# A gated cross-attention and mixture-of-experts block on one core: expert rows added to the rows of x in DRAM by indirect transfers, in place of a store and a gather

## The reference

```python
x = x + tanh(g_xattn) * xattn(layernorm(x), ctx, masks)      # 16 heads, 128 context rows
n = layernorm(x)
probs, idx = top_k(softmax(n @ router), 2)                   # 8 experts, each token takes 2
routed = sum_k probs[k] * (silu(n @ gate[idx[k]]) * (n @ up[idx[k]])) @ down[idx[k]]
shared = (silu(n @ shared_gate) * (n @ shared_up)) @ shared_down
x = x + tanh(g_ffn) * (routed + shared)
```

## The kernel before, in words

| engine | in this order in iteration k |
|---|---|
| SP | load the 128 token numbers of slot k (L405), after the gather of slot k-4 |
| POOL | gather the normed rows of slot k (L514), after PE has transposed slot k-4 |
| PE | transposes of g_h, slot k-3; transposes of the gathered rows, slot k (both L1038); gate and up products, slot k-1; down product, slot k-3 (L1046 to L1048) |
| DVE | g_h_lo, slot k-2; g_lo, slot k (L964); g_y of slot k-3 (L970), the down product times its scale; g_h, its peak and scales, slot k-1 |
| ACT | g_ht, slot k-3; store of g_y of slot k-4 to `y_dram` (expert_rows), L651; g_h_hi, slot k-2; g_hi, slot k; silu, slot k-1 |

## Time and profile before

### The profile page before, as it was taken

One profiled execution on the slowest core, in us unless ns is written; L12 is line 12 of the kernel. 1 busy time (PEld: TensorE's weight loads), 2 busy tenths in 40 slices (PEclk: granted clock), 3 DMA queues, 4 the chain that ended last, 5 costly groups with the idle time before them and its releaser, 6 DMA issues.

```text
span 1155.8 us, 26617 instructions
## 1 busy us (share of the span) xinstructions
PE 1050.2 (91%) x7344; PEld 677.3 (59%) x7345; DVE 822.7 (71%) x2938; ACT 531.4 (46%) x1041; POOL 441.8 (38%) x654
## 2 busy tenths in 40 slices
PE   4699979999999999860899999999999999999997
PEld 3488767777777777660455555555554444444443
DVE  5899868788888888763576666666665666666666
ACT  1366546666666666640444444444443232232322
POOL 3254647676667667442112112112110423232322
PEclk9999889999999999855899999999999999999999
DMA  7555573223323223432233333333332544444543
GB/s 290 197 177 179 131 173 95 93 93 93 93 93 94 94 93 110 101 102 72 74 110 118 115 113 118 118 109 118 118 109 67 185 158 161 157 168 149 169 149 128
DMA packets 76731, 146.96 MB, mean 127 GB/s; under 512 B 20912, under 2 KB 23088, under 8 KB 73872
## 3 DMA queue, kind: packets, MB, share of 16 engines
q1 hardware_dynamic: 46512, 66.01, 20.0%
q10 hardware_dynamic: 17280, 44.83, 10.5%
q0 software_dynamic: 12896, 35.58, 9.9%
HBM read 94.04 MB, written 52.35 MB: 127 GB/s over the span
## 4 chain that ended last, share of the span: by engine, by line
PE 64%; issue 11%; DVE 9%; POOL 8%; ACT 4%; DMA 2%; POOLq 1%; another core or an unknown queue 1%; SPq 0%; DVEq 0%; ACTq 0%
PE bank L1046 15%; PE bank L1047 15%; PE bank L1048 15%; PE bank L1038 8%; PE bank L1090 3%; PE bank L1108 3%; DVE arena L776 3%; POOL arena L467 3%; POOL token_of_row L503 2%; ACT arena L605 1%; DVE arena L865 1%; POOL arena L474 1%; DMA token_of_row<-arena 1%; DVE peak L879 1%; PE bank L1064 1%
## 5 line engine op out<-in xcount | busy, mean ns | idle before, releaser
L1046 PE MATMUL bank<-weights,arena 128*128 (+1 forms) x682 | 259.9, 381 | 2.1 <-ACT arena L647 1.9
L1047 PE MATMUL bank<-weights,arena 128*128 (+1 forms) x682 | 259.8, 381 | 0.0
L1048 PE MATMUL bank<-weights,arena 128*128 (+1 forms) x682 | 259.6, 381 | 0.0
L1038 PE MATMUL bank<-ident,arena 128*128 128x128 f32 (+1 forms) x1592 | 189.4, 267 | 56.1 <-DMA arena<-normed_rows,arena 25.7
L1038 PEld LDWEIGHTS bank<-ident,arena 128*128 128x128 f32 (+1 forms) x1592 | 161.4, 132 | 103.0 <-issue 71.9
L514 POOL DMA_INDIRECT arena<-normed_rows,arena x71 | 67.1, 946 | 254.9 <-PE bank L1038 238.7
L1108 PEld LDWEIGHTS bank<-arena 128*128 128x128 f32 x1024 | 131.7, 198 | 34.3 <-issue 29.5
L1090 PE MATMUL bank<-arena 128*128 128x512 f32 x256 | 138.8, 647 | 5.4 <-DVE arena L776 5.1
L1108 PE MATMUL bank<-arena 128*128 128x33 f32 x1024 | 128.8, 276 | 2.9 <-issue 1.8
L467 POOL TENSOR_TENSOR arena<-arena 128x512 f32<-128x512 f32 x96 | 101.3, 1056 | 76.8 <-DVE arena L776 75.7
L524 POOL DMA_INDIRECT arena<-expert_rows,arena x64 | 62.8, 981 | 173.9 <-DVE arena L998 156.1
(11 more groups left out here) (175 smaller groups left out, 1895.7 us busy)
## 6 DMA issues: line engine op xcount, KB each, us to landing
expert_rows<-arena ACTq DMA_DIRECT2D x71, 256.0 KB, 2.1
arena<-in_x SPq DMA_DIRECT2D x64, 256.0 KB, 3.2
weights<-in_w_gu ACTq DMA_DIRECT2D x8, 1024.0 KB, 4.7
x_rows<-arena SPq DMA_DIRECT2D x32, 256.0 KB
normed_rows<-arena SPq DMA_DIRECT2D x32, 256.0 KB, 4.9
normed_transposed<-arena SPq DMA_DIRECT2D x32, 256.0 KB, 2.3
arena<-normed_transposed SPq DMA_DIRECT2D x32, 256.0 KB, 3.3
arena<-x_rows SPq DMA_DIRECT2D x32, 256.0 KB, 3.4
```

The lines of the kernel that those rows point to most:

```text
L1038: last = t.transpose(dst[:, c * P:(c + 1) * P], src[:, c * P:(c + 1) * P], (ident16 if src.dtype == F16 else ident)[:, :])
L1046: t.matmul(dst, hi[:, rows], w_hi(c), start=(c == 0), stop=False)
L1047: t.matmul(dst, hi[:, rows], w_lo(c), start=False, stop=False)
L1048: last = t.matmul(dst, lo[:, rows], w_hi(c), start=False, stop=(c == chunks - 1))
```

## The change

Three things change together. (1) The list in DRAM has two words a row: token number and weight. Rows that nobody writes hold, in place of zero, one of 288 (SPARE) token numbers beyond the last token, with weight 0; `x1_dram` and `xn_dram` get 288 rows more, which POOL fills with zeros at the start. POOL therefore makes seven stores at the start instead of one. In the attention pass POOL copies the token number into both entries, DVE writes prob * gate beside them at L856 (where it now waits for the scatters of the tile two earlier), and the scatters carry 8 bytes a row. (2) In the expert pass DVE multiplies each row of the down product by its own weight (g_weight: the row's scale times the list's weight), and POOL, in place of ACT's store, adds the 128 rows to the rows of `x1_dram` by an indirect transfer with compute_op add. Each add is issued only once the one before it has landed, since two slots may hold the same token. (3) The last pass gathers nothing: x1 as loaded already holds the expert rows, and one DVE operation makes the result. SP waits for all adds before it loads x1; the five plan operations for row_all go.

```diff
-    x1_dram = nc.dram_tensor("x1_rows", [TOK, E], F32).ap()
-    xn_dram = nc.dram_tensor("normed_rows", [TOK, E], F32).ap()
+    x1_dram = nc.dram_tensor("x1_rows", [TOK + SPARE, E], F32).ap()
+    xn_dram = nc.dram_tensor("normed_rows", [TOK + SPARE, E], F32).ap()
-    list_dram = nc.dram_tensor("token_of_row", [LISTS, 1], I32).ap()
-    y_dram = nc.dram_tensor("expert_rows", [SLOTS * P, E], F32).ap()
+    list_dram = nc.dram_tensor("token_and_weight", [LISTS, 2], I32).ap()
...
@@ SP, expert pass and its end
-                    need(sp, xg_here[u], 16 * j)
+                    need(sp, g_weight_done, s - 3)
+                    need(sp, g_tok_ready, s - 3)
...
+                if it == SLOTS + 2:
+                    for u in range(2):
+                        sp.wait_ge(y_added[u], 16 * ((SLOTS + 1 - u) // 2))
                 if it >= SLOTS:
                     body3((it - SLOTS) // 2, (it - SLOTS) % 2)
@@ POOL, start
+            g.iota(pairs[:, :, 0], [[1, SPARE]], base=TOK, channel_multiplier=0).then_inc(pool_set, 1)
+            g.memset(pairs[:, :, 1], 0).then_inc(pool_set, 1)
+            g.memset(no_x, 0.0).then_inc(pool_set, 1)
...
+            for at in range(TOK, TOK + SPARE, SPARE // 3):
+                pool.dma_start(xn_dram[at:at + SPARE // 3, :], no_x[0:SPARE // 3, :]).then_inc(list_zero, 16)
+                pool.dma_start(x1_dram[at:at + SPARE // 3, :], no_x[0:SPARE // 3, :]).then_inc(list_zero, 16)
+            pool.dma_start(list_dram.rearrange("(p n) a -> p (n a)", p=P), no_rows.bitcast(I32)).then_inc(list_zero, 16)
...
-            pool.wait_ge(list_zero, 16)
+            pool.wait_ge(list_zero, 112)
@@ POOL, attention pass
                     need(pool, rows_out[u], 16 * TOP * j)
-                    g.tensor_copy(tok_i[u], token_no[:, :, :].rearrange("p j b -> p (j b)")[:, bass.ds(n, 1)]).then_inc(tok_ready, 1)
-                    hold(pool, pool_passed, (tok_ready, n + 1), (row_ready, n + 1))
+                    for k in range(TOP):
+                        g.tensor_copy(pairs[:, k, 0:1].bitcast(I32), token_no[:, :, :].rearrange("p j b -> p (j b)")[:, bass.ds(n, 1)]).then_inc(tok_ready, 1)
+                    hold(pool, pool_passed, (tok_ready, group(n, TOP - 1, TOP)), (row_ready, n + 1), (prob_ready, n + 1))
                     for k in range(TOP):
                         g.indirect_dma_start(list_dram, bass.IndirectOffsetOnAxis(ap=row_i[u][:, k:k + 1], axis=0),
-                                             tok_i[u], None).then_inc(rows_out[u], 16)
+                                             entry[u][:, 2 * k:2 * k + 2].bitcast(I32), None).then_inc(rows_out[u], 16)
@@ POOL, expert pass, behind the gather of slot k
+                s, j, u = tile(J, v, 1, 4, SPAN2)
+                if live(s, SLOTS):
+                    hold(pool, pool_passed, (y_added[u % 2], 16 * added_before(s, j, u)))
+                    g.tensor_copy(g_tok[u], id_in[u][:, 0:1].bitcast(I32)).then_inc(g_tok_ready, 1)
+                s, j, u = tile(J, v, 4, 4, SPAN2)
+                if live(s, SLOTS):
+                    hold(pool, pool_passed, (g_y_ready, s + 1), (g_tok_ready, s + 1), (y_added[1 - u % 2], 16 * (2 * j + (u + 1) // 2)))
+                    g.indirect_dma_start(x1_dram, bass.IndirectOffsetOnAxis(ap=g_tok[u].bitcast(U32), axis=0), g_y[u % 2], None,
+                                         compute_op=ALU.add).then_inc(y_added[u % 2], 16)
@@ ACT, expert pass
-                    act.wait_ge(g_y_ready, s + 1)
-                    act.dma_start(y_dram[bass.ds(s * P, P), :], g_y[u]).then_inc(y_out[u], 16)
@@ DVE, attention pass, L856 and L870
-                    d.tensor_scalar(prob_all[:, bass.ds(n7 * TOP, TOP)], r_top[:, 0:TOP], r_inv, None, ALU.mult)
+                    need(dve, rows_out[u7], 16 * TOP * j7)
+                    d.tensor_scalar(entry[u7].rearrange("p (k a) -> p k a", a=2)[:, :, 1], r_top[:, 0:TOP], r_inv, gate[:, 1:2], ALU.mult, ALU.mult).then_inc(prob_ready, 1)
...
-                    d.tensor_copy(row_list[:, bass.ds(n8 * TOP, TOP)], row_f)
@@ DVE, expert pass, L970 and behind L982
-                    need(dve, y_out[u], 16 * j)
-                    d.tensor_scalar(g_y[u], bank[6 + u][:, :], size, w_back[:, 2:3], ALU.mult, ALU.mult).then_inc(g_y_ready, 1)
+                    dve.wait_ge(g_weight_done, s + 1)
+                    need(dve, y_added[u], 16 * j)
+                    d.tensor_scalar(g_y[u], bank[6 + u][:, :], g_weight[(v - 3) % 4], None, ALU.mult).then_inc(g_y_ready, 1)
...
+                    dve.wait_ge(id_here[(v - 1) % 4], 16 * (s4 + 1))
+                    d.scalar_tensor_tensor(g_weight[(v - 1) % 4], size, w_back[:, 2:3], id_in[(v - 1) % 4][:, 1:2], ALU.mult, ALU.mult).then_inc(g_weight_done, 1)
@@ DVE, last pass: L993, L996 and L998 go; L1002 becomes
+                    d.scalar_tensor_tensor(f_out[u], bank[7][:, :], f_back[u], f_x1[u], ALU.mult, ALU.add).then_inc(f_out_ready, 1)
```

More of the change, by code:

```diff
@@ L35 @@
 LISTS = (NX + 1) * REGION
+SPARE = LISTS // P
 EPS = 1e-5
@@ L178, in build @@
         row_i = [carve(TOP).bitcast(U32) for _ in range(2)]
-        tok_i = [carve(1).bitcast(I32) for _ in range(2)]
+        entry = [carve(2 * TOP) for _ in range(2)]
+        no_rows, no_x = free_early[:, 0:2 * SPARE], free_early[:, 2 * SPARE:2 * SPARE + E]
         top[0] = 0
@@ L184, in build @@
         swd = carve(SD).bitcast(F16).rearrange("p (a n) -> p a n", a=2)
-        id_in = [carve(1).bitcast(I32) for _ in range(4)]
+        id_in = [carve(2) for _ in range(4)]
         xg = [carve(E) for _ in range(4)]
@@ L197, in build @@
         g_y = [carve(E) for _ in range(2)]
+        g_tok = [carve(1).bitcast(I32) for _ in range(4)]
+        g_weight = [carve(1) for _ in range(4)]
         PASS2_END = top[0]
         SCORES_END = EC * E + B * EC * HG * T + B * H * (D + 1) + 2 * H * T
-        PLAN = NX * NT + 3 * NX + NX * NX + 2 * SLOTS * NX + 2 * SLOTS + NT * TOP * NX
+        PLAN = NX * NT + 3 * NX + NX * NX + 2 * SLOTS * NX + 2 * SLOTS
         top[0] = SCORES_END - PLAN
@@ L210, in build @@
         expert_f, row_sf = carve(SLOTS), carve(SLOTS)
-        later = carve(NT * TOP * (NX - 1))
-        row_slots = carve(NT * TOP)
         swd_raw = carve(SD)
@@ L218, in build @@
         f_x1 = [carve(E) for _ in range(2)]
-        f_idx = [[carve(1).bitcast(U32) for _ in range(TOP)] for _ in range(2)]
-        f_y = [[carve(E) for _ in range(TOP)] for _ in range(2)]
         f_act = [carve(DS) for _ in range(2)]
@@ L513, in body2, with added_before @@
                     hold(pool, pool_passed, (gt_done, s - 3), (id_here[u], 16 * (j + 1)))
-                    g.indirect_dma_start(xg[u], None, xn_dram, bass.IndirectOffsetOnAxis(ap=id_in[u], axis=0)).then_inc(xg_here[u], 16)
-            def body3(J, v):
-                n, j, u = tile(J, v, 1)
-                if live(n, NT):
-                    need(pool, f_y_here[u], 16 * TOP * j)
-                    for k in range(TOP):
-                        g.tensor_copy(f_idx[u][k], row_all[:, bass.ds(n * TOP + k, 1)]).then_inc(f_idx_ready, 1)
-                    hold(pool, pool_passed, (f_idx_ready, n * TOP + TOP), (f_c2_done, n - 1))
-                    for k in range(TOP):
-                        g.indirect_dma_start(f_y[u][k], None, y_dram, bass.IndirectOffsetOnAxis(ap=f_idx[u][k], axis=0)).then_inc(f_y_here[u], 16)
-            def beside2(it):
-                if it == SLOTS + 1:
-                    for u in range(2):
-                        pool.wait_ge(y_out[u], 16 * ((SLOTS + 1 - u) // 2))
-                if it >= SLOTS:
-                    body3((it - SLOTS) // 2, (it - SLOTS) % 2)
-            pipeline(pool, body2, SLOTS, LAG2, SPAN2, beside=beside2)
-            pipeline(pool, body3, NT, LAG3, start=LAG2)
+                    g.indirect_dma_start(xg[u], None, xn_dram, bass.IndirectOffsetOnAxis(ap=id_in[u][:, 0:1].bitcast(U32), axis=0)).then_inc(xg_here[u], 16)
+                s, j, u = tile(J, v, 1, 4, SPAN2)
[7 more added lines that the diff above has]
+                                         compute_op=ALU.add).then_inc(y_added[u % 2], 16)
+            def added_before(s, j, u):
+                return 2 * j + u // 2 - 1
+            pipeline(pool, body2, SLOTS, LAG2, SPAN2)
         @block.scalar
@@ L942, in _ @@
             d.tensor_copy(slot_expert[:, :], expert_f).then_inc(plan_ready, 1)
-            l3 = later.rearrange("p (r e) -> p r e", e=NX - 1)
-            link(d.tensor_tensor(l3, row_list[:, :].unsqueeze(2).to_broadcast([P, NT * TOP, NX - 1]),
-                                 region_at[:, 1:NX].unsqueeze(1).to_broadcast([P, NT * TOP, NX - 1]), ALU.is_ge))
-            link(d.tensor_tensor(l3, l3, ahead[:, 0:NX - 1].unsqueeze(1).to_broadcast([P, NT * TOP, NX - 1]), ALU.mult))
-            link(d.tensor_reduce(row_slots, l3, AX.X, ALU.add))
-            link(d.tensor_tensor(row_slots, row_list[:, :], row_slots, ALU.subtract))
-            link(d.tensor_copy(row_all[:, :], row_slots))
```

(4 more changed lines are left out.)

42 lines of the change are left out of this document (14 added, 28 removed).

## The result

The changed kernel takes 1322.43 us (median of 4 runs, 1320.21 to 1337.72) where the kernel before took 1161.17 on the same chip: ratio 1.143, 95% interval 1.135 to 1.151 (a fifth run, of 1329.59 us, counts in it; the medians' own ratio is 1.139). So it is 161 us slower; 92 were predicted. The profiled execution took 1337.72 us, span 1336.0, the longest of the four.

| stretch, by its marks | before | after | difference | predicted |
|---|---|---|---|---|
| start to first list load | 538.59 | 545.66 | +7.1 | +23 (Parts 4 and 5) |
| expert pass, to PE's first round of the last pass | 355.3 | 523.25 | +168 | +69 (Parts 1 to 3) |
| last pass and tail | 261.9 | 267.1 | +5.2 | +0.5 (Part 6) |

The account below looks back on a forecast made before the run. PE bounds the expert pass, where POOL's queue, which feeds PE, would decide. 69 + 4 + 10 + 6 + 3 + 3.5 - 3 = 92.5 on 1157.6 us gives 1250, median 1253 us; range 1195 to 1400.

Parts of the forecast that it names:

- Part 4: Attention pass: extra token copy, DVE's new wait at L856, later end of the pass; +4, +10 and +6 us.
- Part 5: Start: more zero stores and a longer list go out beside the load of wq; 0 to 4.2, taken as +3 us.
- Part 1: Expert pass, POOL's queue: gather behind add, a loop of 11.05 us over two rounds; 5.6 a round taken, +69 us.
- Part 2: Expert pass: each add waits for the previous one's landing, 4.2 us; a round of 5.1, not the limit.
- Part 3: Expert pass, smaller things: ACT's lost stores, DVE's added operations, list load's new wait, dropped plan operations; nothing.
- Part 6: Step to the last pass: PE waits for f_x behind all adds, +3.5 us; tail loses DVE operations, -3.
- Rival A: Expert pass: the adds themselves limit, landing above 4.7 us; 1339 us at a landing of 6; chance 0.27.
- Rival B: Expert pass: granted clock falls to 1.2 GHz; 201 us in place of 69, 1385 us; chance 0.06.
- Rival C: Attention pass: new wait at L856 costs 3 us a tile, 90 in place of 10; 1333 us; chance 0.06.
- (a): Attention pass: POOL copies the token number twice a tile, 0.16 us more each; +4 us.
- (b): Attention pass: DVE waits at L856 for the scatters of the tile two earlier, about 0.35 us a tile; +10 us.
- (c): End of the attention pass: last scatter, POOL's drain and the expert pass's start move later by 1 to 7 us; +6.

Follow-up runs that it names:

- run 6: The changed kernel with four more matmuls a round, whose result nobody reads, ahead of PE's wait for the gathered tile; 1310.07 us, ratio 1.117.
- run 3: The changed kernel with POOL's gather issued ahead of the add, and the token-number copy between them; 1266.88 us, ratio 1.084.
- run 2: The changed kernel with the indirect scatter overwriting rows of x1 instead of adding to them; 1280.49 us, ratio 1.096.
- run 4: The changed kernel with POOL's gather issued ahead of the add, and the token-number copy last; 1252.98 us, ratio 1.070.
- run 9: The changed kernel with the seven zero stores issued after tile 0's mask, and DVE instead of POOL waiting for them; 1319.6 us, ratio 1.136.
- run 1: The changed kernel with ACT's plain store to a separate buffer in place of POOL's adds; 1193.63 us, ratio 1.019.
- run 8: As run 1, with POOL also copying the list entry, so SP's list load no longer waits for DVE's g_weight; 1167.45 us, ratio 1.004.
- run 10: The kernel before, with separate buffers for row and token numbers of the attention pass's last two tiles; 1175.5 us, ratio 0.9997.
- run 11: The changed kernel with adds alternating between two arrays, POOL's order gather, add, copy, list entry copied, spare rows' zeros late; 1169.23 us, ratio 1.004.

## Why the prediction was right in direction and short in size

The time lay in the stated range, but the forecast itself (rounds of 5.1 to 5.9 us, 1215 to 1285 us, chance 0.56) did not come true; the upper part of the range had been given to rivals A, B and C, and of these only B, the clock, came true in part. So the range held, but not for the reasons given for its upper half. Part 4's 20 us, which didn't come, hid some of the miss.

- **Part 1, queue order: the mechanism right, the sum mis-sized, and this is where most of the miss lies.** Forecast 4.7 + 0.8 + 0.9 + 1.25 + 3.4 = 11.05 for two rounds; measured 5.28 + 0.75 + 0.87 + 1.91 + 4.32 = 13.13 (697.80 to 710.93). The failed terms are "the add's issue and the gap behind it" (the issue took 1.60, not 0.95), the gather's landing (4.32, not 3.4) and PE's piece (5.28; 0.39 of it is a gap before L1036 where the gather comes last). Half of 13.13 is 6.56 a round, and with the clock back the rounds are just that, 6.57 (run 6): 135 us in place of 69. The order's worth is 1.117 to 1.084 (runs 6 and 3), and 1.143 to 1.084 with the clock that comes back with it. The landing is 3.4 again when the scatter overwrites (run 2): it is the accumulating transfer just ahead of the gather that makes it longer.
- **Part 2, add after add: mis-sized, and "not the limit" right by luck.** It said L = 4.2, a round of 5.1. L is 4.9, and I had left out that POOL's copy stands between landing and issue. So the loop is 6.0, above the 5.6 that Part 1 was given, and would have been the limit if Part 1's sum had been right. Since that is 6.56, Part 2's loop delays every second add (by up to 0.25 us at full clock, by 1 us and more where the clock is low) and splits the pairs, but it is on the chain in few rounds. Rival A (0.27) had its condition fulfilled, L above 4.7, and its 5.8 a round is near what the kernel does once the gather stands first (5.93 and 5.78, runs 3 and 4), but it isn't what bounds the changed kernel. By the Trainium skill's rule (Collectives: The Full Stack, "The bandwidth ceiling: the fold count and why AG ≠ RS ≠ AR"), that an add costs a second source read and no more, the plain scatter's 2.8 and 0.84 for another pass would give 3.6; the runs show 4.9, so here the measurement decides against it (0.6 of the difference is POOL's longer issue, 1.60 against 1.0).
- **Rival B, the clock: 0.06 was far too low, its price too high.** The pass ran at 0.89 of 2.4 GHz on average, not at 1.2 GHz; runs 6 and 9 put the cost at 16 to 32 us in place of 132. In after PE waited for gathers up to 4.4 us, in run 2 1.7 on average and 2.0 at most in every second round (0.91). In the even rounds of runs 3 and 4 it waited 0.6 and 0.5 us on average, 1.8 at most, in nearly every round, and the clock kept 0.99 and 1.00. That a wait in each round can bring the slow clock back, as the Trainium skill has it (TensorE: Matmul & The Clock Gate, "HAM oscillation — how this bites in real kernels"), agrees with after and run 2, and not with the short waits of runs 3 and 4.
- **Part 3, "nothing", was wrong but hidden.** The list load, "still some three rounds ahead", had lost those three rounds: behind g_weight it closes a loop of 4.85 us a round. Alone it costs 1.5% (runs 1 and 8); in the changed kernel, in rounds of 7.0, nothing: from 600 to 1040 us all 62 gathers start 0.3 us behind the add.
- **Part 4: too high.** (a) and (b), +14: from the first scatter to the last, after takes 413.56 us, before 412.44 (117.64 to 530.08), and the eight executions with after's code in that pass 412.1 to 419.7. L858 waits only four times in the whole pass, 10.3 us, nine tenths of it in the last three tiles. (c), +6: it is inside that difference too. The 8-byte scatters of after land in 3.9 us (median); of the 4-byte ones only two crowded landings are known, 9.5 and 7.3, so whether the size or the crowd makes the difference stays open. Rival C falls with this. Run 10 says that the waits at the end aren't the limit; the drain follows the scatters.
- **Part 5: right**, +3 forecast, +4.1 at wq, removed by run 9. It is 6.6 by the first scatter, but that place moves by 4.7 us between executions of the same code (122.5 to 127.2), so the further 2.5 may be nothing.
- **Part 6: small.** PE's wait for f_x was 6.4 us where 3.5 were forecast. The last four adds still followed each other by 5.5 to 5.8 us after PE had done its rounds; the tail gave back about 1.2 of its 3, for the stretch is 5.2 longer in all.

Put together for the profiled execution: from the first add to the last it takes 491.2 us, where before takes 324.6 from the first store of expert rows to the last. Of the 167 us, 32 are the clock and 135, by run 6, the loops, Part 1's nearly alone. That this one execution is 15 us longer than the median of its kernel fits the clock as well: its mean granted clock is 0.913, the other four runs have 0.923 to 0.931, and run 9, at 0.931, is 16 us shorter in this stretch.

## What to carry to other kernels

When a transfer joins a queue that also feeds the bound engine, write down, for each instruction behind it, what it waits for and how many rounds it then leads; a lead of four rounds can shrink to none while PE's busy share in the pass falls only from 100% to 96% (before and run 1, 600 to 850 us). A wait that is "still three rounds ahead" has to be followed round its loop to the same instruction, and the loop's length divided by its rounds. Two loops through one queue don't add up: the longer one per round sets the mean, and long and short rounds in turn can come from one loop that spans two. Serial read-modify-write transfers to one array are limited by their landing once nothing longer stands before them (runs 3 and 4); alternating between two arrays, summed later where another engine has time, took that limit away here.

## What the runs showed of the hardware

- An accumulating indirect transfer of 128 rows of 2 KB into DRAM held POOL 1.60 us and landed in 4.9; the same scatter that overwrites 1.0 and 2.8; the gather 0.95 to 1.0 and 3.4 to 3.6 (before, runs 1, 2 and 8), 4.2 right behind an add (after), 3.7 in run 11. Adds to two arrays in turn, 4.63 us apart, landed in 4.8; with more overlap than some 0.2 us there are only a few (2.95 us apart at the closest, 4.5 to 5.3).
- Indirect scatters of 128 entries landed in 3.9 us (median) at 8 bytes. Where the last ones no longer waited for buffers, POOL's drain behind them was longer: 7.86 us before, 15.05 in run 10, one execution each.
- PE at 78% busy with waits of up to 4.4 us had a granted clock of 0.90 (0.94 in another execution of the same code); four matmuls a round that nobody reads, 88% busy, brought 0.99 and made the kernel 2% faster. Waits of about 1.7 us in every second round left 0.91 (run 2); waits of 0.5 to 0.6 in nearly every round left 0.99 and 1.00 (runs 3, 4).
- Between runs with the same code in the attention pass, its end moved by 9 us (543.6 to 552.6), so effects of a few us there need a place in the trace, not a ratio.
